# Attention scores from three products instead of four, the last of them split over two halves of the array

## What is computed

```python
h, d = (NUM_HEADS, HEAD_DIM)          # 8, 64
scale = d ** (-0.5)
q = _proj(x, Wq, bq).reshape(B, h, d, H * W).transpose(0, 1, 3, 2)
k = _proj(x, Wk, bk).reshape(B, h, d, H * W).transpose(0, 1, 3, 2)
scores = jnp.einsum('bhnd,bhmd->bhnm', q, k) * scale
attn = jax.nn.softmax(scores, axis=-1)
out = jnp.einsum('bhnm,bhmd->bhnd', attn, v)
```

## Time and profile before

| | |
|---|---|
| median of 3 runs | 3360.12 us (3359.72 to 3362.19) |
| the profiled execution | 3358.84 us, of which the span is 3357.0 us |
| PE busy | 3154.9 us (94%) |
| DVE busy | 2319.4 us (69%) |
| ACT busy | 2003.8 us (60%) |
| attention | from about 50 to 2480 us |
| mean granted clock of PE | 0.979 |

### The profile page before, as it was taken

How to read it: one execution, slowest core, us unless ns; L and a number is a source line. 1 busy time by engine, 2 the same in 40 slices (tenths; PEclk the granted TensorE clock), 3 DMA queues, 4 the chain that set the end, 5 groups by cost and what they waited for, 6 DMA issues and landing times. The chain is left out here.

```text
span 3357.0 us, 51875 instructions
## 1 busy us (share of the span) xinstructions
PE 3154.9 (94%) x18562; PEld 2696.9 (80%) x18562; DVE 2319.4 (69%) x3649; ACT 2003.8 (60%) x3833; POOL 1294.3 (39%) x1536
## 2 busy tenths in 40 slices
PE   6999999999999999999999999999944999999998
PEld 5888888788878888887888888888833888888886
DVE  5877687678768776875877677667766556555553
ACT  4876678478748856883887578478821333333332
POOL 1335234423523352343335234523432444444443
PEclk9999999999999999999999999999977999999999
DMA  6012111310220131112103211310132565655654
GB/s 219 26 51 101 52 51 39 113 52 26 82 96 26 51 109 51 44 51 101 52 27 101 77 41 40 111 39 26 39 114 61 135 133 126 142 136 120 149 136 59
DMA packets 108907, 268.82 MB, mean 80 GB/s; under 512 B 13456, under 2 KB 21648, under 8 KB 97936
## 3 DMA queue, kind: packets, MB, share of 16 engines
q1 hardware_dynamic: 80016, 198.80, 17.6%
q0 software_dynamic: 28672, 67.13, 11.2%
HBM read 158.40 MB, written 73.92 MB: 69 GB/s over the span
## 5 line engine op out<-in xcount | busy, mean ns | idle before, releaser
L727 DVE TENSOR_TENSOR PT<-ring,PT 128x512 fp32r<-128x512 f32 x1024 | 675.7, 685 | 230.8 <-ACT PT L475 221.8
L877 PE MATMUL O<-PT,V 128*128 128x256 f32 x4096 | 677.0, 290 | 0.0
L669 DVE TENSOR_REDUCE nmax<-S 128x1 f32<-128x1024 f32 x512 | 619.4, 1210 | 78.1 <-PE S L834 78.0
L395 POOL TENSOR_SCALAR rinv_bc<-ones,rinv 128x128 f32<-128x128 f32 x512 | 303.6, 605 | 934.3 <-DVE rinv L735 931.5
L845 PE MATMUL ring<-ident,prob 128*128 128x128 f32 x4096 | 617.2, 274 | 38.6 <-DVE qs L662 19.4
L475 ACT ACTIVATE PT<-ring 128x512 fp32r<-128x512 f32 x1024 | 582.1, 598 | 84.9 <-PE ring L845 70.5
L877 PEld LDWEIGHTS O<-PT,V 128*128 128x128 f32 x4096 | 577.7, 189 | 39.1
L466 ACT ACTIVATE prob<-S,nmax 128x1024 f32<-128x1024 f32 x512 | 571.7, 1117 | 56.3 <-DVE nmax L669 56.3
L834 PE MATMUL S<-kd,qs 128*128 128x512 f32 x2048 | 594.7, 414 | 3.4 <-DVE qs L662 2.3
L845 PEld LDWEIGHTS ring<-ident,prob 128*128 128x128 f32 x4096 | 460.3, 140 | 83.8 <-issue 70.4
L834 PEld LDWEIGHTS S<-kd,qs 128*128 128x128 f32 x2048 | 349.1, 189 | 55.5 <-ACT prob L466 2.8
(11 more groups left out here) (115 smaller groups left out, 3840.7 us busy)
## 6 DMA issues: line engine op xcount, KB each, us to landing
kd<-kd SPq DMA_DIRECT2D x128, 256.0 KB, 3.7
wraw<-w_dram SPq DMA_DIRECT2D x32, 1024.0 KB, 6.7
wqk<-wqk_split SPq DMA_DIRECT2D x24, 1024.0 KB, 4.8
xt<-x_dram SPq DMA_DIRECT2D x16, 1024.0 KB, 7.5
PT<-wv_split SPq DMA_DIRECT2D x7, 2048.0 KB, 8.2
oT<-x_dram SPq DMA_DIRECT2D x24, 512.0 KB, 3.6
out_dram<-oT SPq DMA_DIRECT2D x48, 256.0 KB, 8.3
n_rows<-oT SPq DMA_DIRECT2D x48, 256.0 KB, 2.3
```

Source lines behind the costliest of these rows:

```text
L395: last_bc = nc.gpsimd.tensor_scalar(rinv_bc[:, k % 2, j, :], ones[:, :], rinv[:, 2 * k + j:2 * k + j + 1], None, ALU.mult)
L669: nc.vector.tensor_reduce(nmax[:, s:s + 1], S[:, s % 2, :], AX.X, ALU.max, negate=True).then_inc(max_done, 1)
L727: nc.vector.tensor_tensor(PT[:, 1, here[0], here[1], here[2]], ring[:, k % 2, :].rearrange("p (m q) -> p m q", m=4), PT[:, 0, here[0], her ...
L877: last_mm = nc.tensor.matmul(O[:, m % 2, 0:QC], V[:, t, head // 2, 2 * (head % 2):2 * (head % 2) + 2, :].rearrange("p h d -> p (h d)"), PT ...
```

## The change

Scores are formed in three steps. The weights [q_hi; q_hi] meet [k_hi; k_lo] on all 128 rows, which gives q_hi times both parts of k, one matmul for each half of the keys. The missing part is q_lo times k_hi, with a contraction over 64 rows. It is made by two matmuls of 64 rows each: the first half of the keys on one half of the array's rows, the second half on the other. For the second of them the second half of k_hi must lie on the other 64 partitions, in the new tile `k_far`. (The product q_lo times k_lo, which the kernel before included, is left out.)

```diff
-        qs = sb("qs", [P, 2, N], F32R)
-        kd = sb("kd", [P, 2, 2, N], F32R)
+        q_hi = sb("q_hi", [P, 2, N], F32R)
+        q_lo = sb("q_lo", [P, 2, N], F32R)
+        k_both = sb("k_both", [P, 2, N], F32R)
+        k_far = sb("k_far", [P, 512], F32R)
...
+            def duplicate_q(j, p):
...
-                        sp.dma_start(kd[other, odd, :, cols].bitcast(F32),
-                                     kd[rows, odd, :, cols].bitcast(F32)).then_inc(k_dup, 16)
+                        for q in (q_hi, q_lo):
+                            sp.dma_start(q[other, odd, cols].bitcast(F32),
+                                         q[rows, odd, cols].bitcast(F32)).then_inc(q_dup, 16)
...
-                        dst = kd[rows, odd, 0, cols] if r < 2 else qs[rows, odd, cols]
+                        rows, other = slice(D * odd, D * odd + D), slice(D * (1 - odd), D * (1 - odd) + D)
+                        if r == 3:
+                            nc.scalar.activation(k_far[other, :], ring[rows, k % 2, :], ACT.Identity,
+                                                 bias=bqk[rows, 1, p:p + 1])
+                        dst = (q_hi if r < 2 else k_both)[rows, odd, cols]
...
-                        hi, lo = ((kd[rows, odd, 0, cols], kd[rows, odd, 1, cols]) if r < 2 else
-                                  (qs[rows, odd, cols], qs[other, odd, cols]))
+                        hi, lo = ((q_hi[rows, odd, cols], q_lo[rows, odd, cols]) if r < 2 else
+                                  (k_both[rows, odd, cols], k_both[other, odd, cols]))
...
-                             [(w[:, 2 * (1 - r // 2) + h, c, :], nT[:, l, c, (r % 2) * 512:(r % 2) * 512 + 512])
+                             [(w[:, 2 * (r // 2) + h, c, :], nT[:, l, c, (r % 2) * 512:(r % 2) * 512 + 512])
...
-                    pe.wait_ge(k_dup, j * (64 * PAIRS) + 64 * (s // UP) + 64)
+                    pe.wait_ge(q_dup, j * (128 * PAIRS) + 128 * (s // UP) + 128)
...
                 for m in range(2):
-                    for l in range(2):
-                        last_mm = nc.tensor.matmul(S[:, s % 2, 512 * m:512 * m + 512], qs[:, odd, i * P:(i + 1) * P],
-                                                   kd[:, odd, l, 512 * m:512 * m + 512],
-                                                   start=(l == 0), stop=(l == 1))
+                    nc.tensor.matmul(S[:, s % 2, 512 * m:512 * m + 512], q_hi[:, odd, here],
+                                     k_both[:, odd, 512 * m:512 * m + 512], start=True, stop=False)
+                nc.tensor.matmul(S[:, s % 2, 0:512], q_lo[rows, odd, here], k_both[rows, odd, 0:512],
+                                 start=False, stop=True)
+                last_mm = nc.tensor.matmul(S[:, s % 2, 512:1024], q_lo[other, odd, here], k_far[other, :],
+                                           start=False, stop=True)
```

More of the change, by code:

```diff
@@ L172, in attention @@
         wqk_in = sem("wqk_in")
-        k_dup = sem("k_dup")
+        q_dup = sem("q_dup")
         t_out = [sem(f"t_out{i}") for i in range(2)]
@@ L248, in staged @@
             if j == 0:
-                return kd[:, h, :, :].rearrange("p l n -> p (l n)")
-            return qs[:, :, :].rearrange("p a n -> p (a n)") if h == 0 else wqk[:, :, :, :].rearrange(
+                return (q_hi if h == 0 else q_lo)[:, :, :].rearrange("p a n -> p (a n)")
+            return k_both[:, :, :].rearrange("p a n -> p (a n)") if h == 0 else wqk[:, :, :, :].rearrange(
                 "p w k c -> p (w k c)")
@@ L313, in _ @@
             load_pair(1)
-            duplicate_k(0, 0)
+            duplicate_q(0, 0)
             def image(b, last):
@@ L320, in image @@
                 for p in range(1, PAIRS):
-                    duplicate_k(b, p)
+                    duplicate_q(b, p)
                     if p < PAIRS - 1 or not last:
@@ L346, in image @@
                 if not last:
-                    duplicate_k(b + 1, 0)
+                    duplicate_q(b + 1, 0)
                 sp.wait_ge(affT_copied, b * 2 + 2)
@@ L458, in high_of_proj @@
                     for odd in range(2):
-                        rows = slice(D * odd, D * odd + D)
-                        dst = kd[rows, odd, 0, cols] if r < 2 else qs[rows, odd, cols]
+                        rows, other = slice(D * odd, D * odd + D), slice(D * (1 - odd), D * (1 - odd) + D)
[3 more added lines that the diff above has]
+                        dst = (q_hi if r < 2 else k_both)[rows, odd, cols]
                         nc.scalar.activation(dst, ring[rows, k % 2, :], ACT.Identity,
-                                             bias=bqk[rows, 1 - r // 2, p:p + 1]).then_inc(ring_hi if odd else even_hi, 1)
+                                             bias=bqk[rows, r // 2, p:p + 1]).then_inc(ring_hi if odd else even_hi, 1)
             def exponentials(j, s):
@@ L659, in low_of_proj @@
                         rows, other = slice(D * odd, D * odd + D), slice(D * (1 - odd), D * (1 - odd) + D)
-                        hi, lo = ((kd[rows, odd, 0, cols], kd[rows, odd, 1, cols]) if r < 2 else
-                                  (qs[rows, odd, cols], qs[other, odd, cols]))
+                        hi, lo = ((q_hi[rows, odd, cols], q_lo[rows, odd, cols]) if r < 2 else
+                                  (k_both[rows, odd, cols], k_both[other, odd, cols]))
                         last_lo = nc.vector.scalar_tensor_tensor(
-                            out=lo, in0=ring[rows, k % 2, :], scalar=bqk[rows, 1 - r // 2, p:p + 1],
+                            out=lo, in0=ring[rows, k % 2, :], scalar=bqk[rows, r // 2, p:p + 1],
                             in1=hi.bitcast(F32), op0=ALU.add, op1=ALU.subtract)
@@ L828, in scores @@
                     pe.wait_ge(ring_lo, j * RING + ring_proj(s // UP, 3) + 1)
-                    pe.wait_ge(k_dup, j * (64 * PAIRS) + 64 * (s // UP) + 64)
+                    pe.wait_ge(q_dup, j * (128 * PAIRS) + 128 * (s // UP) + 128)
                 if s >= 2:
                     pe.wait_ge(exp_done, j * UNITS + s - 1)
+                rows, other = slice(D * odd, D * odd + D), slice(D * (1 - odd), D * (1 - odd) + D)
+                here = slice(i * P, (i + 1) * P)
                 for m in range(2):
-                    for l in range(2):
-                        last_mm = nc.tensor.matmul(S[:, s % 2, 512 * m:512 * m + 512], qs[:, odd, i * P:(i + 1) * P],
-                                                   kd[:, odd, l, 512 * m:512 * m + 512],
-                                                   start=(l == 0), stop=(l == 1))
+                    nc.tensor.matmul(S[:, s % 2, 512 * m:512 * m + 512], q_hi[:, odd, here],
[4 more added lines that the diff above has]
+                                           start=False, stop=True)
                 last_mm.then_inc(s_filled, 1)
```

1 line of the change is left out of this document (removed).

## The result

The changed kernel takes 3495.82 us in the median of four runs (3473.22 to 3519.45) against 3359.92 us for the kernel before: the ratio is 1.0406, with a 95% interval of 1.0323 to 1.0488. The forecast was 3522 us and slower, its range 3410 to 3580. The runs of the changed kernel lie up to 46 us apart, those of the kernel before 5 us; this turned out to be part of the answer. Each run's span times its mean granted clock (0.968, 0.958, 0.956 and 0.969 of full speed) gives 3361 to 3368 us, so nearly all of the 46 us go with the clock. Later, on another chip, five runs gave 3490.47 us (3482.84 to 3493.89) and a ratio of 1.0400 (1.0385 to 1.0415).

A forecast was written before the change was run, and what follows sets the result against it. PE was taken to set the pace, with ACT close behind. 119 us for the half-row units plus 43 for the copies made 162 on a 3357 us span, 3519, and 3522 as the median; range 3410 to 3580.

The forecast's parts named there:

- The change of shape: Into and out of each unit's half-row pair: 0.42 us instead of 0.23, so 0.19 us per change, two a unit.
- The case against it: Transposes with 16 columns are followed by a scores load 0.11 us later, without a wait: the lower end, zero.
- Inside the pair: The second half-row matmul starts 0.11 us after the first, bounds 0 and 0.23; a unit loses 0.26 us.
- rival 1: Both half-row loads start at once; a unit loses 0.15 us, giving 3471 us; chance 0.24.
- How many units pay: Of 512 units, 24 at pair ends and 32 at image starts are covered; 456 lose 0.26 us each, 119 us.
- the first: that PE alone sets the pace: Dense attention: PE is busy 5.70 us a block, ACT 5.35; PE savings beyond 0.35 go unseen, all losses count.
- k_far: Two extra ACT copies delay the last low part: 33 us at 24 pair starts, 10 at image starts, together 43.
- The duplicates: SP issues four transfers after r = 1 instead of two; they stay hidden by about 1.8 us, at no cost.
- the 162 us of the sum: Loss on the span: 119 us for the units that pay plus 43 us for the copies on ACT.
- Rival 2: No drain at the half-row loads: scores cost three matmuls, 80 us saved less 43, giving 3323 us; chance 0.10.

The follow-up runs named there:

- The half-row step alone: The changed kernel with the copies into k_far made only once, at the first pair of the first image: 3409.55 us, ratio 1.0151.
- three matmuls: Changed kernel with one whole-array matmul replacing the half-row pair, second half of keys without third product, copies made once: 3341.00 us, ratio 0.9957.
- the copies alone with the wait filled: The kernel before plus the two copies on ACT and eight extra whole-array matmuls in PE's wait at pair starts within images: 3393.23 us.
- the copies alone: The kernel before, four whole-array matmuls per unit, with only the two copies on ACT added, into an unread tile: 3428.92 us, ratio 1.0200.
- The changed kernel with its wait filled: The full changed kernel plus eight extra whole-array matmuls in PE's wait at each pair start within an image: 3450.17 us, ratio 1.0272.

## Why the prediction was right, and where it was not

**The change of shape: right.** The wait of 0.32 us before the first half-row load was read from the router's products and came out as 0.32. The open load of 0.11 on both sides came too. The case against it, the transposes with 16 columns of weights, did not carry over. "TensorEngine Tiling (Array Packing)" of the Trainium skill, Key Properties, said that a change of mode drains; the trace after agrees, with 0.38 us of idle time in each of 512 units.

**Inside the pair: wrong, the mechanism of rival 1 right.** The forecast put the second half-row matmul 0.11 us behind the first, from two loads that shared rows. They start 0.00 to 0.01 us apart, and the kernel with both on the same rows shows that they run together. The unit loses 0.17 us, not 0.26, and a late block takes 6.04 us, not 6.2. With 456 units that is 78 us instead of 119. The second property on the same page of the Trainium skill, that different tiles load and multiply in parallel, agrees with this row.

**How many units pay: wrong.** The forecast had 456. The half-row step alone cost 50 us by the medians, so about 290 units of 0.17 paid. The step that failed is the first: that PE alone sets the pace, read from four blocks of one pair. In the late blocks of the first three pairs of an image both units pay in full, 5.69 to 6.04. Early in the second and third pair a block took 5.83 us before and 5.83 with three matmuls as well, so the loop set the pace there, and it became 6.05. In the last pair of an image the last three blocks (6.20, 6.21 and 5.68 us before) stayed as long in all three kernels, and in the blocks of 6.20 PE had waited 0.3 us for the ring before; the dense part of that pair grew by 0.7 us instead of 1.8. And the three units around a pair start paid 0.1 us together. Reading a busy share of 100% as "the bound" overstates a loss, and a gain much more.

**k_far: right in size.** The forecast had 43 us, of which 33 at the pair starts; the copies alone with the wait filled show 34 in all, of which 33 at the pair starts, 1.37 us at each of the 24. What the image starts got, 10 us by the forecast, isn't settled: with the copies alone they took 6 us more, but the half clock there also lasted 47.8 us instead of 34.1, which can account for it.

**The duplicates: right.** Twice the DMAs on SP were never waited for.

**The clock: missing.** A term of 40 to 46 us that the sum did not have. The profile before had a wait of 0.80 us at full clock, and the forecast made it 2.2 us without asking what the clock would do.

So in place of the 162 us of the sum the runs gave 50 for the half-row step where 119 stood, 34 for the copies where 43 stood, and some 40 to 46 for the clock where nothing stood. The changed kernel with its wait filled shows 7 us more than the two parts add up to. That too can be the clock: by the mean clocks of the runs an estimate gives 8 us, and in the profiles the half clock at the image starts lasted 27 us longer than the parts would make it. The direction and the two causes that were named are right; that the time is near the forecast is luck, since a term 69 us too large met one of over 40 us that was missing. Rival 2, a kernel without the drain, was put at 3323 us and measured at 3406: its gain was sized by ACT's busy time, where the loop through the ring was the limit, and its clock fell too.

## What to carry to other kernels

Two half-array matmuls did run side by side here, but the way into that shape and the way out of it cost about 0.2 us each after 512-column matmuls. One saved matmul of 0.23 us doesn't pay for both. An engine that is busy all the time may share its pace with a loop through the other engines: before a saving is counted, look for buffers that come free just in time, and check whether the work to be saved is in that loop at all. And if a change makes TensorE wait longer in one place, look at the granted clock behind it; here a filler of useless matmuls was worth 36 to 40 us.

## What the runs showed of the hardware that was not expected

Two half-row weight loads on different rows start together and cost 0.11 us as one does; on the same rows the second matmul costs its full 0.23 us. Idle times of 0.3, 0.8 and 1.2 us at the pair starts left the granted clock at 1.00; idle times of 2.1 to 2.2 us were followed by a fall to half speed at 23 and 24 of 24 pair starts with whole-array scores, and at 13 and 15 of 24 with half-row ones, worth 1.0 to 1.5 us for each pair start in the mean of all 24. The runs of the changed kernel differ by 46 us, and its two profiles have the falls at different sets of pair starts.
